# Two-layer graph network: the second layer in steps of eight rows, pairs of rows mixed at once, one-hots per row, four slots for gathered features

## The chip, the cores and the metric

One core of one Trainium2 chip. The metric is the device time of one execution in microseconds, the median of the runs shown. The engines are PE (TensorE, matmuls), DVE (VectorE), ACT (ScalarE), POOL (GpSimd, which here issues the indirect gathers) and SP (SyncE, which issues plain DMAs).

## What is computed

There are 8192 nodes with 128 features and 262144 edges, sorted by target node `dst` (the targets are denser at low numbers). The first layer sums weighted neighbour features, multiplies by W and normalizes. The second one, the subject here, forms for each edge a tensor product of the source node's features with nine edge attributes, sums the products by target node, adds the node's features and normalizes:

```python
edge_index = jnp.stack([src, dst])
x = _layernorm(x + _L0_gnn_ref(x, src, dst, edge_weight, L0_gnn_W), axis=-1)
x = _layernorm(x + _L1_gnn_ref(x, edge_index, edge_attr_9, w0, w1, w2, w3, w4), axis=-1)

# in _L1_gnn_ref: for each of five paths (i1, i2, io)
seg = jnp.einsum('uvw,ijk,eui,evj->ewk', weights[k], _W3J[k], x1s, x2s) * _NORM[k]
out = out.at[:, e:f].add(seg.reshape(E, mo * (2 * lo + 1)))
# then
out = jax.ops.segment_sum(summand, j, num_segments=x.shape[0])
return out / float(np.sqrt(NUM_NEIGHBORS))
```

The product is linear in the features and in each of the nine attributes, so the kernel first sums feature times attribute per target node and attribute, and then multiplies each of the nine sums by a 128x128 matrix (`g.mix[:, m, :]`), which holds the weights and the coupling coefficients.

## The kernel before

The edges are cut into 128 rows of 16 tiles of 128 edges. Function `layer1` runs an outer loop over passes (one pass with these inputs) and in it over the rows. For each row:

- POOL issues 16 indirect DMAs (L1558), one for each tile: 128 feature rows of 512 bytes each land in `feat[z]`, z being one of two row slots. It waits for the ids, which ACT copies to integers for each half row (L1599), and, through `half_summed`, for PE to have read the same half of the row before last.
- SP loads the row's attributes (`attr_in`, L1521), and PE turns them in nine narrow transposes into PSUM (`attr_t`, L1639).
- DVE makes, for each half row of 8 tiles, a one-hot of the target within a window of 16 nodes (`hot`, L1758) and its product with the attributes (`attr_hot`, L1763).
- PE takes the tiles in quads of four. For each quad it zeroes a PSUM bank by a matmul with a zero operand (L1666), and then accumulates one matmul for each tile, features against one-hot times attributes (`quad`, L1673), at a column offset that is read from a table. The last one of a half increments `half_summed`.
- DVE adds the quads of each half to the row's sums in SBUF (`group[z]`, L1784), ACT clears the group for the row after next (L1596).
- PE mixes the nine sums of a row (`mixed`, 9 matmuls of 192 columns, L1688), and DVE adds the result at the row's place to `g.acc` (L1790). This is done in `add_row` while the next row runs.

An f32 matmul leaves two records in the trace, a transpose one. Rows 0 to 111 are in loops of two rows (`Fori(0, EARLY // 2)`); rows 112 to 127 are unrolled, and in 112 to 126 a batch of 512 finished nodes is done beside the edges: four transposes into `y` (L1682) between PE's two halves, which wait for the last row's `add_row`; then DVE's `measure` (L1798 to L1813) and ACT's normalization and store (L1577 to L1584). The last batch follows the last row. Each engine runs its own program in order; the order of the work is that of the code, and semaphores tie the engines together.

Of the kernel before, what the change touches and what calls it, by code (L numbers as in the profile page):

```python
# [89 lines left out]
ROW_SLOTS = 2  # L90
# [36 lines left out]
def constants(n_nodes):  # L127
# [29 lines left out]
    c[:, C_BEGUN] = np.where(done >= 0, BATCH * P * np.minimum(done + 1, n_batches - 1), 0)  # L157
# [18 lines left out]
def gnn_kernel(nc, x, src, dst, attr, weight, w_lin, w_tp, consts, out, tables, x1):  # L176
# [10 lines left out]
    with ExitStack() as ctx:  # L187
# [6 lines left out]
        g.src_col = sb("src_col", [P, g.TN + ROW_SLOTS * ROW_TILES], F32)  # L194
# [41 lines left out]
def setup(nc, g, src, dst, weight, w_lin, w_tp, consts):  # L236

    RN, TN = g.RN, g.TN
    with ExitStack() as ctx:
# [75 lines left out]
        def _(dve):  # L315
# [76 lines left out]
            nc.vector.tensor_copy(g.src_col[:, TN:TN + ROW_SLOTS * ROW_TILES], g.src_col[:, 0:ROW_SLOTS * ROW_TILES])  # L392
# [1024 lines left out]
def layer1(nc, g, x1, attr, out):  # L1417

    RN, TN = g.RN, g.TN
    H, Q, R = HALF_TILES, QUAD_TILES, ROW_TILES  # L1420
    with ExitStack() as ctx:
# [6 lines left out]
        zero_bf = sb("zero_bf", [P, NA * QUAD_WIN], BF16)  # L1428
        off_f = sb("off_f", [P, TN], F32)
        tile_offs = sb("tile_offs", [P, TN // Q, Q - 1], I32)  # L1430
        row_offs = sb("row_offs", [P, RN + 1, Q], I32)
# [6 lines left out]
        quad = ctx.enter_context(nc.psum_tensor("quad", [P, Q, 512], F32))  # L1438
# [11 lines left out]
        EARLY = RN - g.NB  # L1450

        zero_made = sem("zero_made")
# [3 lines left out]
        feat_in = [[sem(f"feat_in{z}_{q}") for q in range(R // Q)] for z in range(ROW_SLOTS)]  # L1456
        attr_here = [sem(f"attr_here{z}") for z in range(2)]
        first_turned = sem("first_turned")
        half_summed = sem("half_summed")
        hot_step = sem("hot_step")  # L1460
        hot_made = sem("hot_made")
        quad_added = sem("quad_added")
        group_zero = sem("group_zero")
        acc_added = sem("acc_added")
# [36 lines left out]
        SUMMED = 2 * RN + 1  # L1501

        def pass_begun(w):

            return w * SUMMED + 2 * ROW_SLOTS

        def all_mixed(w):

            return pass_begun(w) + SUMMED

        def summed(w, r, h):

            return w * SUMMED + r * 2 + (h + 1 + 2 * ROW_SLOTS)

        @block.sync
        def _(sp):
            attr_rows = attr.rearrange("(r t e) m -> r t (e m)", t=R, e=P)

            def load_attr(row, z):

                sp.dma_start(attr_in[z][:], attr_rows[bass.ds(row, 1)].squeeze(0)).then_inc(attr_here[z], 16)  # L1521

            load_attr(0, 0)
            sp.wait_ge(first_turned, 1)
# [7 lines left out]
            with passes(sp) as w:  # L1532
                with sp.Fori(0, EARLY // 2) as i:
                    for z in range(2):
                        sp.wait_ge(half_summed, summed(w, i * 2, z * 2 - 4))
                        load_attr(i * 2 + (z + 1), 1 - z)
                load_x(w, 0)
                for r in range(EARLY, RN):
                    sp.wait_ge(half_summed, summed(w, r - 2, 0))
                    load_attr((r + 1) % RN, (r + 1) % 2)  # L1540
# [3 lines left out]
            for z in range(2):  # L1544
                sp.wait_ge(attr_here[z], n_loads * (8 * RN) + 16 * (1 - z))
# [3 lines left out]
        def _(pool):  # L1549
            with passes(pool) as w:  # L1550
                with pool.Fori(0, RN // ROW_SLOTS) as i:
                    for z in range(ROW_SLOTS):
                        for h in range(2):
                            pool.wait_ge(ids_made, w * (RN * 2) + i * (2 * ROW_SLOTS) + (z * 2 + h + 1))
                            pool.wait_ge(half_summed, summed(w, i * ROW_SLOTS, (z - ROW_SLOTS) * 2 + h))
                            pool.sem_inc(g.turn, 1)
                            for t in range(h * H, h * H + H):
                                pool.indirect_dma_start(  # L1558
                                    feat[z][:, t, :], None, x1,
                                    bass.IndirectOffsetOnAxis(ap=ids[z][h][:, t % H:t % H + 1], axis=0),  # L1560
                                ).then_inc(feat_in[z][t // Q], 16)
                for z in range(ROW_SLOTS):
                    for q in range(R // Q):
                        pool.wait_ge(feat_in[z][q], 16 * Q * (RN // ROW_SLOTS))
                pool.wait_ge(half_summed, all_mixed(w))
                pool.sem_inc(g.turn, 1)
                pool.inc_swdge_sem(sum(feat_in, []), [16 * Q * (RN // ROW_SLOTS)] * (ROW_SLOTS * R // Q), mode="sub")
                pool.sem_inc(landings_cleared, 1)
# [3 lines left out]
        def _(act):  # L1572
            def normalize(w, e):
# [15 lines left out]
            for z in range(ROW_SLOTS):  # L1589
                for h in range(2):  # L1590
                    cols = z * R + h * H
                    nc.scalar.copy(ids[z][h][:], g.src_col[:, cols:cols + H]).then_inc(ids_made, 1)
            with passes(act) as w:
                def clear_and_copy(r, z, e=None):
                    act.wait_ge(half_summed, summed(w, r, -2))
                    nc.scalar.memzero(group[z][:]).then_inc(group_zero, 1)  # L1596
                    for h in range(2):
                        act.wait_ge(half_summed, summed(w, r, h))
                        nc.scalar.copy(ids[z][h][:], g.src_col[:, bass.ds(r * R + (ROW_SLOTS * R + h * H), H)]  # L1599
                                       ).then_inc(ids_made, 1)  # L1600
                        if h == 0 and e is not None:
                            normalize(w, e)

                with act.Fori(0, EARLY // 2) as i:
                    for z in range(2):
                        clear_and_copy(i * 2 + z, z)
                for r in range(EARLY, RN):
                    clear_and_copy(r, r % 2, batch_of(r))
# [17 lines left out]
        def _(pe):  # L1626
            pe.sem_inc(half_summed, 2 * ROW_SLOTS)
            pe.sem_inc(landings_cleared, 1)
            pe.sem_inc(quad_added, R // Q)
            pe.sem_inc(acc_added, 2)  # L1630

            def turn_attr(v, v_half, z):

                pe.wait_ge(attr_here[z], v_half * 16 + 16)
                pe.wait_ge(hot_made, v * 2 + 1)
                pe.sem_inc(g.turn, 1)
                edges = attr_in[z][:].rearrange("t (e m) -> t e m", m=NA)
                for m in range(NA):
                    last = nc.tensor.transpose(attr_t[:, z, m * R:(m + 1) * R], edges[:, :, m],  # L1639
                                               g.cst[0:R, C_IDENT:C_IDENT + R])  # L1640
                return last
# [254 lines left out]
```

## Time and profile before

| | us |
|---|---|
| median of 3 runs | 4115.09 (4114.18 to 4115.81) |
| the profiled execution, its span | 5011.3 |
| PE busy | 3029.2 (60%) |
| POOL busy | 2759.7 (55%) |
| DVE busy | 2089.5 (42%) |
| ACT busy | 1176.6 (23%) |

The profiled execution's own time is its span; no other time of it is given, and it is longer than the timed runs. Up to about 500 us the kernel sorts and prepares, then runs the first layer until 1802, a normalization until 1860, and the second layer from there. Busy shares are averages over these stages.

### The profile page before, as it was taken

To read this page: it belongs to the slowest core of one execution; us is meant where nothing else is said; L and a number is where in the kernel's file an instruction comes from. 1 tells how busy PE (TensorE), PEld (TensorE's weight loads), DVE (VectorE), ACT (ScalarE), POOL (GpSimd) and SP (SyncE) were. 2 spreads that over 40 slices of the span, in tenths; PEclk is the share of its full clock that TensorE was granted. 3 is DMA by queue.
4 is the path that set the end of the run, shared out by engine and by line. 5 is a ranking of instruction groups with operands and counts; after the bars stand their busy time and mean duration, and the time that the engine had idled before them with its cause. 6 is when DMAs were issued, how large, how long until landed. Compare 5 with 4: busy or idle time off the path is not lost.

```text
span 5011.3 us, 63448 instructions
## 1 busy us (share of the span) xinstructions
PE 3029.2 (60%) x18004; PEld 2599.8 (52%) x18006; DVE 2089.5 (42%) x4613; ACT 1176.6 (23%) x2104; POOL 2759.7 (55%) x2887
## 2 busy tenths in 40 slices
PE   2100788888888864555555555555556555555666
PEld 1000778788887863444444444444445444444555
DVE  8999565565565661222222222222222222222333
ACT  5443444444444440000000000000000000000111
POOL 4000555555555536666666666666666666666664
PEclk6555899999999976777777777777777777777666
DMA  1001222222222231111111111111111111111221
GB/s 49 5 11 41 75 71 75 71 71 76 72 71 71 71 96 47 46 47 46 46 46 46 46 47 46 46 46 46 46 47 47 46 47 45 46 46 55 66 66 46
DMA packets 117978, 267.07 MB, mean 53 GB/s; under 512 B 52225, under 2 KB 52369, under 8 KB 116769
## 3 DMA queue, kind: packets, MB, share of 16 engines
q0 software_dynamic: 92080, 191.02, 13.1%
q1 hardware_dynamic: 21234, 66.99, 3.9%
q10 hardware_dynamic: 4608, 8.39, 0.4%
q8 instruction: 25, 0.41, 0.0%
q14 instruction: 31, 0.25, 0.0%
HBM read 251.19 MB, written 8.72 MB: 52 GB/s over the span
## 4 chain that ended last, share of the span: by engine, by line
another core or an unknown queue 34%; PE 11%; issue 10%; DVE 6%; DVEq 2%; ACT 0%; ACTq 0%
PE quad L1673 5%; PE mixed L1688 4%; DVE group L1784 3%; DVE hot L1758 1%; PE quad L1666 1%; PE attr_t L1639 1%; DVE acc L1790 1%; DVEq L1769 1%; DVE attr_hot L1763 0%; DVEq L1784 0%; DVEq L1758 0%; DVEq L1777 0%; DVEq L1780 0%; DVEq L1761 0%
## 5 line engine op out<-in xcount | busy, mean ns | idle before, releaser
L1558 POOL DMA_INDIRECT feat<-x,ids x2048 | 1940.6, 948 | 1181.8 <-issue 615.8
L1784 DVE TENSOR_TENSOR group<-group,quad 128x504 f32 (+1 forms) x512 | 347.3, 678 | 2301.9 <-remote 2167.5
L1134 POOL DMA_INDIRECT l_feat<-in_x,id_of x768 | 737.4, 960 | 916.5 <-ACT w_of L827 368.7
L1673 PE MATMUL quad<-attr_hot,feat 128*128 128x144 f32 x4096 | 842.8, 338 | 547.7 <-issue 544.3
L1673 PEld LDWEIGHTS quad<-attr_hot,feat 128*128 128x128 f32 x4096 | 661.0, 219 | 737.5 <-issue 736.4
L1688 PE MATMUL mixed<-group,mix 128*128 128x192 f32 x2304 | 691.1, 486 | 577.9 <-DVE group L1784 577.9
L1688 PEld LDWEIGHTS mixed<-group,mix 128*128 128x128 f32 x2304 | 650.5, 305 | 622.7 <-issue 556.8
L1599 ACT CAST ids<-src_col 128x8 int32 (+1 forms) x256 | 50.3, 197 | 2746.0 <-remote 2525.4
L1208 PE MATMUL got<-x_near,far_w 128*128 128x128 bf16 x4224 | 341.0, 220 | 160.3 <-issue 148.6
L1208 PEld LDWEIGHTS got<-x_near,far_w 128*128 128x128 bf16 x4224 | 278.7, 98 | 206.4 <-issue 192.1
L1036 DVE TENSOR_SCALAR keys<-swap,src_of,w_of 128x184 f32<-128x184 f32 x1024 | 308.2, 373 | 127.9 <-PE l_pre L1227 122.0
L1036 DVE TENSOR_SCALAR w_row<-swap,src_of,w_of 128x184 f32<-128x184 f32 x1024 | 311.8, 376 | 112.7 <-PE l_pre L1227 108.4
L1763 DVE TENSOR_TENSOR attr_hot<-hot,attr_t 128x1152 f32<-128x1152 f32 x256 | 346.5, 1354 | 9.0
L853 ACT COPY pad<-got 128x640 f32<-128x640 f32 x256 | 176.0, 688 | 595.3 <-remote 450.1
L1227 PE MATMUL l_pre<-w_row,pad 128*128 128x184 f32 x1280 | 297.4, 352 | 0.0
L1227 PE MATMUL l_pre<-keys,pad 128*128 128x184 f32 x1280 | 284.4, 339 | 4.2 <-issue 4.2
L1666 PE MATMUL quad<-zero_bf 1*128 1x504 bf16 x512 | 204.5, 399 | 109.2 <-issue 109.1
L1227 PEld LDWEIGHTS l_pre<-w_row,pad 128*128 128x128 f32 x1280 | 247.0, 216 | 0.0
L1227 PEld LDWEIGHTS l_pre<-keys,pad 128*128 128x128 f32 x1280 | 233.0, 206 | 6.0 <-issue 5.6
L839 ACT ACTIVATE far_keys<-place,turn_f 128x384 bf16<-128x384 bf16 (+2 forms) x384 | 229.1, 630 | 6.5 <-DMA place<-table 6.4
L1227 PE MATMUL l_pre<-w_row,l_feat 128*128 128x184 f32 x768 | 212.6, 362 | 12.6 <-ACT pad L853 7.8
L1227 PE MATMUL l_pre<-keys,l_feat 128*128 128x184 f32 x768 | 203.7, 348 | 20.4 <-ACT pad L853 16.8
(249 smaller groups left out, 2929.8 us busy)
## 6 DMA issues: line engine op xcount, KB each, us to landing
place<-table SPq DMA_DIRECT2D x64, 640.0 KB
feat<-x,ids POOLq DMA_INDIRECT x2048
l_feat<-in_x,id_of POOLq DMA_INDIRECT x768
attr_in<-in_edge_attr SPq DMA_DIRECT2D x129, 72.0 KB
norm_x<-in_x SPq DMA_DIRECT2D x16, 256.0 KB, 2.7
x<-norm_z ACTq DMA_DIRECT2D x16, 256.0 KB, 2.4
x_t<-x SPq DMA_DIRECT2D x15, 256.0 KB
out<-z_t ACTq DMA_DIRECT2D x15, 256.0 KB
```

The lines of the kernel that those rows point to most:

```text
L839: nc.scalar.activation(rest_far[r][:, cols[r]], placed_at(s, j, cols[r]), ACT.Abs, bias=not_wanted[r]).then_inc(far_made, 2 // len(cols))
L853: nc.scalar.copy(rows, got[j % 2][:, 0:NF[j] * P]).then_inc(msg_made, 1)
L1036: made = nc.vector.tensor_scalar(hot_of[(j % 2) * GROUP + i], iota[KIND[j][i]], src_of[s % 2][:, c:c + 1], w_of[s % 2][:, c:c + 1], ALU.is ...
L1134: pool.indirect_dma_start(feat[:, landing, :], None, x, bass.IndirectOffsetOnAxis(ap=id_of[s % 2][:, c:c + 1], axis=0)).then_inc(feat_in[l ...
L1208: last = nc.tensor.matmul(got[z][:, cols], hot, rows, start=(n_done == 0), stop=(n_done == len(products) - 1))
L1227: made = nc.tensor.matmul(pre[:, s % 2, bass.ds(places[i], WIN0)], rows, hot_of[(j % 2) * GROUP + i], start=False, stop=(j == GROUPS - 1 a ...
L1558: pool.indirect_dma_start(feat[z][:, t, :], None, x1, bass.IndirectOffsetOnAxis(ap=ids[z][h][:, t % H:t % H + 1], axis=0),).then_inc(feat_ ...
L1666: nc.tensor.matmul(quad[:, q, 0:NA * QUAD_WIN], zero_bf[0:1, 0:P], zero_bf[0:1, :], start=True, stop=False, skip_group_check=True)
L1673: last = nc.tensor.matmul(bank[:, :, bass.ds(places[t % H], WIN)], feat[z][:, t, :], attr_hot[h][:, t % H, :, :], start=False, stop=(t % Q ...
L1688: last = nc.tensor.matmul(mixed[:, 0:GROUP_WIN], g.mix[:, m, :], group[z][:, m, :], start=(m == 0), stop=(m == NA - 1))
L1763: nc.vector.tensor_tensor(attr_hot[h][:], hot[:].unsqueeze(2).to_broadcast(s4), by_tile[:, h * H:h * H + H, :].unsqueeze(3).to_broadcast(s ...
L1784: nc.vector.tensor_tensor(to, to, quad[:, q, 0:NA * QUAD_WIN].rearrange("p (m n) -> p m n", m=NA), ALU.add).then_inc(quad_added, 1)
```

## The change

Only the second layer changes.

- **Slots and ids.** `feat` has four row slots for two, and one semaphore for each half row (it had one for each quad). The ids are copied for four rows at once. POOL's loop has eight rows.
- **Attributes.** They are loaded for eight rows in one DMA (128 partitions), turned by nine transposes of 128 columns in eight rows (attribute 8 first, in the step of row 2, the other eight in that of row 4), and copied by ACT from PSUM to SBUF (`attr_e`, `attr_next`).
- **One-hots.** One pair of DVE instructions for each row, with all 16 tiles, made two rows ahead into one of two buffers.
- **Zeroing.** ACT clears the two PSUM banks of a half (`clear_half`) as soon as DVE has added them; PE's matmuls with the zero operand are gone, and PE waits for `quad_zero`, once in a half.
- **Mixing.** A group holds two rows; nine matmuls of 384 columns mix both, in the loop after the next row's two halves, in the unrolled rows right after an odd row. DVE adds them with two adds (`add_pair`).
- **Unrolled rows.** The transposes of an even batch wait for all earlier rows, those of an odd batch for one row less (`turn_nodes`), and the node count in `C_BEGUN` is rounded to pairs.

```diff
-ROW_SLOTS = 2
+ROW_SLOTS = 4
+OCTET = 8
+TURN_ROW = 4
+START_LAG = 3
...
-        ids = [[sb(f"ids{z}_{h}", [P, H], I32) for h in range(2)] for z in range(ROW_SLOTS)]
-        feat = [sb(f"feat{z}", [P, R, D], F32) for z in range(ROW_SLOTS)]
-        attr_in = [sb(f"attr_in{z}", [R, P * NA], F32) for z in range(2)]
-        hot = sb("hot", [P, H, WIN], F32)
-        attr_hot = [sb(f"attr_hot{h}", [P, H, NA, WIN], F32) for h in range(2)]
-        group = [sb(f"group{z}", [P, NA, GROUP_WIN], F32) for z in range(2)]
+        ids = [sb(f"ids{b}", [P, O // 2 * R], I32) for b in range(2)]
+        feat = [sb(f"feat{z}", [P, R, D], F32) for z in range(S)]
+        attr_in = sb("attr_in", [O * R, P * NA], F32)
+        attr_e = sb("attr_e", [P, NA, O * R], F32)
+        attr_next = sb("attr_next", [P, O * R], F32)
+        hot = sb("hot", [P, R, WIN], F32)
+        attr_hot = [sb(f"attr_hot{z}", [P, R, NA, WIN], F32) for z in range(2)]
+        group = [sb(f"group{z}", [P, NA, 2, GROUP_WIN], F32) for z in range(2)]
...
+            def clear_half(h):
+
+                nc.scalar.memzero(quad[:, 2 * h:2 * h + 2, 0:NA * QUAD_WIN]).then_inc(quad_zero, 1)
...
+            def half_row(w, r, h, z, n_fill):
+
+                u = w * RN + r
+                places = tile_places(r, h)
+                pe.wait_ge(quad_zero, u * 2 + (h + 1))
+                if h == 0:
+                    pe.wait_ge(hot_made, u + 2)
+                pe.wait_ge(feat_in[z % S][h], n_fill * (16 * H) + 16 * H)
+                pe.sem_inc(g.turn, 1)
+                for t in range(h * H, h * H + H):
+                    bank = quad[:, t // Q, 0:NA * QUAD_WIN].rearrange("p (m n) -> p m n", m=NA)
+                    last = nc.tensor.matmul(bank[:, :, bass.ds(places[t % H], WIN)], feat[z % S][:, t, :],
+                                            attr_hot[z % 2][:, t, :, :], start=False, stop=(t % Q == Q - 1),
+                                            skip_group_check=True)
+                last.then_inc(half_summed, 1)
...
+            def mix(n, side):
+
+                pe.wait_ge(quad_added, n * 8 + 8)
+                pe.wait_ge(acc_added, n * 2 + 2)
+                pe.sem_inc(g.turn, 1)
+                to = mixed[:, 0:2 * GROUP_WIN].rearrange("p (a n) -> p a n", a=2)
+                for m in range(NA):
+                    last = nc.tensor.matmul(to, g.mix[:, m, :], group[side][:, m, :, :], start=(m == 0),
+                                            stop=(m == NA - 1))
+                last.then_inc(pair_mixed, 1)
+
+            def turn_nodes(w, u, e):
+
+                pe.wait_ge(acc_added, u + 2 - e % 2)
...
                 for r in range(EARLY, RN):
...
+                    half_row(w, r, 0, r, r // S)
+                    if batch_of(r) is not None:
+                        turn_nodes(w, w * RN + r, batch_of(r))
+                    half_row(w, r, 1, r, r // S)
+                    if r % 2 == 1:
+                        mix(w * PAIRS + r // 2, r // 2 % 2)
+                    turn_next(w * OCTETS + (r // O + 1), r % O)
...
+            def add_pair(n, starts):
+
+                dve.wait_ge(pair_mixed, n + 1)
+                for half, at in enumerate(starts):
+                    dve.wait_ge(acc_added, n * 2 + (half + 2))
+                    to = g.acc[:, bass.ds(at, GROUP_WIN)]
+                    nc.vector.tensor_tensor(to, to, mixed[:, half * GROUP_WIN:(half + 1) * GROUP_WIN],
+                                            ALU.add).then_inc(acc_added, 1)
```

How the instructions stand, by engine. First PE before, in the unrolled rows, from the last quad of row 113 through its mix and the transposes of the attributes to the transposes of finished nodes in row 114 (`ISA` and `REGISTER_ALU` are register work and waits):

```order
L1666 MATMUL quad<-zero_bf 128x504
L1673 MATMUL quad<-attr_hot,feat 128x9x16
...
L1688 MATMUL mixed<-group,mix 128x192 x9
L1635 ISA
L1639 MATMUL attr_t<-cst,attr_in 128x16 x9
L1650 TENSOR_LOAD tile_offs
L1665 ISA
L1666 MATMUL quad<-zero_bf 128x504
...
L1682 MATMUL y<-cst,acc 128x128 x4
```

The same place of PE after the change, from the transposes of finished nodes in row 115 to the mix of rows 114 and 115 and the start of row 116:

```order
L1749 MATMUL y<-cst,acc 128x128 x4
L1710 TENSOR_LOAD tile_offs
L1720 REGISTER_ALU
L1727 MATMUL quad<-attr_hot,feat 128x9x16
...
L1739 MATMUL mixed<-group,mix 128x384 x9
L1710 TENSOR_LOAD tile_offs
L1720 ISA
L1722 REGISTER_ALU
L1727 MATMUL quad<-attr_hot,feat 128x9x16
```

The zeroing matmuls and the narrow transposes are gone from every row, and a mix of 384 columns stands in every second row where one of 192 stood in each. In DVE's program, two rows of the loop after the change (an even row's one-hots, then the odd row):

```order
L1843 TENSOR_TENSOR hot<-cst,dst_col 128x256
L1847 TENSOR_TENSOR attr_hot<-hot,attr_e 128x2304
...
L1871 TENSOR_TENSOR group<-group,quad 128x9x56
L1878 ISA
L1880 ISA
L1880 TENSOR_TENSOR acc<-acc,mixed 128x192
L1878 REGISTER_ALU
L1880 ISA
L1880 TENSOR_TENSOR acc<-acc,mixed 128x192
```

Both adds into `acc` stand between the two halves of the odd row, and the one-hots are one pair of instructions for each row, where there were two.

## Rows read from the trace of the kernel before

**Rows 1.** The page's head: the span of the profiled execution, one core
```profile
span 5011.3 us, 63448 instructions
```

**Rows 2.** Windows (us, then busy us and instructions by engine, clock, DMA): first layer, second layer's loop
```profile
600.00:1700.00 1100.00, 941.24 (x8170) 886.13 (x8169) 658.23 (x2247) 536.86 (x1101) 630.86 (x658) 0.93 0.22 72
...
1970.00:4628.00 2658.00, 1537.73 (x6879) 1259.54 (x6879) 659.73 (x996) 220.55 (x328) 1658.59 (x1754) 0.71 0.16 47
```

**Rows 3.** Groups in 1970 to 4628: count, busy us, mean ns, idle before and its releasers
```profile
L1558 POOL DMA_INDIRECT feat<-x,ids x1754 | 1659.2, 946 | 999.7 <-issue 515.1 <-ACT ids L1599 303.9 <-PE quad L1673 180.8
...
L1784 DVE TENSOR_TENSOR group<-group,quad 128x504 f32 (+1 forms) x438 | 296.9, 678 | 1998.3 <-remote 1969.2
L1763 DVE TENSOR_TENSOR attr_hot<-hot,attr_t 128x1152 f32<-128x1152 f32 x219 | 296.4, 1354 | 7.6
L1596 ACT ACTIVATE group<-group 128x1728 uint32<-128x1728 uint32 x109 | 179.1, 1643 | 12.2 <-issue 12.2
L1666 PE MATMUL quad<-zero_bf 1*128 1x504 bf16 x437 | 169.3, 387 | 99.2 <-issue 99.1
...
L1758 DVE TENSOR_TENSOR hot<-cst,dst_col 128x128 f32<-128x128 f32 x219 | 62.3, 284 | 0.0
...
L1790 DVE TENSOR_TENSOR acc<-acc,mixed 128x192 f32 x110 | 38.3, 348 | 0.0
```

**Rows 4.** Timeline, POOL, one pause: start us, us, instruction, idle before it
```profile
3217.86 0.95 POOL L1558 DMA_INDIRECT feat<-x,ids  x1 [4.50 <-ACT ids L1599]
...
3219.11 0.95 POOL L1558 DMA_INDIRECT feat<-x,ids  x1 [0.30 <-issue]
```

**Rows 5.** Timeline, PE and DVE, the same row
```profile
3205.00 1.25 PE L1673 MATMUL quad<-attr_hot,feat 128*128 128x144 f32 x8
...
3209.34 0.38 PE L1673 MATMUL quad<-attr_hot,feat 128*128 128x144 f32 x1 [1.13 <-issue]
...
3212.15 0.57 PE L1666 MATMUL quad<-zero_bf 1*128 1x504 bf16 x1 [2.44 <-issue]
...
3216.69 1.49 DVE L1784 TENSOR_TENSOR group<-group,quad 128x504 f32<-128x504 f32 x2 [17.77 <-remote]
```

**Rows 6.** Timeline, POOL's last issue and the last two mixes
```profile
4968.58 0.94 POOL L1558 DMA_INDIRECT feat<-x,ids  x1 [0.30 <-issue]
...
4982.92 4.63 PE L1688 MATMUL mixed<-group,mix 128*128 128x192 f32 x18 [1.77 <-DVE group L1784]
...
4987.48 1.20 PE L1639 MATMUL attr_t<-cst,attr_in 16*128 16x16 f32 x9
...
4990.32 1.25 PE L1673 MATMUL quad<-attr_hot,feat 128*128 128x144 f32 x8
...
4991.70 1.49 DVE L1784 TENSOR_TENSOR group<-group,quad 128x504 f32<-128x504 f32 x2 [7.25 <-PE quad L1673]
...
4991.81 1.25 PE L1673 MATMUL quad<-attr_hot,feat 128*128 128x144 f32 x8
...
4996.75 6.12 PE L1688 MATMUL mixed<-group,mix 128*128 128x192 f32 x18 [2.20 <-DVE group L1784]
```

**Rows 7.** The page's costliest groups: the first layer's gathering matmuls
```profile
L1208 PE MATMUL got<-x_near,far_w 128*128 128x128 bf16 x4224 | 341.0, 220 | 160.3 <-issue 148.6
```

**Rows 8.** The tile feat: POOL's issues, ns min/median/max, first and last start
```profile
L1558 POOL DMA_INDIRECT feat<-x,ids x2048: 942/947/2177, 1859.7 to 4968.6; - x187
```

**Rows 9.** Timeline, PE and DVE in an unrolled row
```profile
4968.79 1.25 PE L1673 MATMUL quad<-attr_hot,feat 128*128 128x144 f32 x8
...
4973.89 1.10 PE L1682 MATMUL y<-cst,acc 128*128 128x128 f32 x4 [3.85 <-DVE acc L1790]
4975.21 0.69 DVE L1798 TENSOR_TENSOR z_t<-x_t,y 128x512 f32<-128x512 f32 x1
...
4976.12 2.29 PE L1673 MATMUL quad<-attr_hot,feat 128*128 128x144 f32 x8
...
4978.03 0.16 DVE L1813 SCALAR_TENSOR_TENSOR shift<-mv,rstd 128x4 f32<-128x4 f32 x1
```

More of the change, by code:

```diff
@@ L1543, in _ @@
             n_loads = sp.value_load(g.n_pass[0:1, 1:2], min_val=1, max_val=g.PASSES1)
-            for z in range(2):
-                sp.wait_ge(attr_here[z], n_loads * (8 * RN) + 16 * (1 - z))
+            sp.wait_ge(attr_here, n_loads * (16 * OCTETS) + 32)
             sp.sem_inc(loads_ended, 1)
@@ L1588, in _ @@
                 act.sem_inc(stored[s], 16)
[L1589 to L1592, printed above, removed]
-            with passes(act) as w:
[L1594 to L1606, printed above, removed]
+            for b in range(2):
+                copy_ids(b, b * (O // 2 * R))
@@ L1692, in _ @@
+                        half_row(w, r, h, j, n_fill)
+                    if j % 2 == 0 and not (first and j == 0):
+                        mix(w * PAIRS + o * (O // 2) + (j - 2) // 2, (j - 2) // 2 % 2)
+                    turn_next(w * OCTETS + o + 1, j)
                 pe.wait_ge(landings_cleared, w + 1)
                 pe.sem_inc(g.turn, 1)
-                with pe.Fori(0, EARLY // 2) as i:
-                    for z in range(2):
-                        row(i * 2 + z, i, z, w * (RN // 2) + i + z)
@@ L1833, in _, with next_hots @@
-                dve.wait_ge(first_turned, 1)
-                hots(w * RN, 0, 0, 0, pass_begun(w))
-                hots(w * RN, 0, 1, 0, pass_begun(w))
-                row(0, 0, first=True)
-                row(0, 1)
-                with dve.Fori(1, EARLY // 2) as i:
-                    row(i, 0)
-                    row(i, 1)
-                for r in range(EARLY, RN):
-                    row(r // 2, r % 2, last=(r == RN - 1))
+                def next_hots(o, j):
+                    if (j + 2) % O == 0:
+                        dve.wait_ge(attr_out, w * (2 * OCTETS) + o * 2 + 4)
+                    r = o * O + (j + 2)
+                    hots(w * RN + r, r, (j + 2) % O, j % 2)
@@ new lines, in row @@
+                def row(o, j, first=False):
+                    r = o * O + j
+                    n = w * PAIRS + o * (O // 2) + j // 2
+                    if j % 2 == 0 or first and j == 1:
+                        starts, offs = [], load_places(r * Q + 1, Q - 1)
+                    else:
+                        begin, *offs, end = load_places(r * Q, Q + 1)
+                        starts = [begin, end]
+                    offs = quad_places(offs)
+                    add_quads(w, r, n, j // 2 % 2, j % 2, 0, offs)
+                    if starts:
+                        add_pair(n - 1, starts)
+                    add_quads(w, r, n, j // 2 % 2, j % 2, 1, offs)
+                    next_hots(o, j)
@@ new lines, in end_pair @@
+                def end_pair(n, r):
+                    begin, *_, end = load_places((r + START_LAG) * Q, Q + 1)
+                    add_pair(n, [begin, end])
+                dve.wait_ge(attr_out, w * (2 * OCTETS) + 2)
+                for r in range(2):
+                    hots(w * RN + r, r, r, r)
+                for j in range(O):
+                    row(0, j, first=True)
+                with dve.Fori(1, LOOPED) as o:
+                    for j in range(O):
+                        row(o, j)
```

295 lines of the change are left out of this document (166 added, 129 removed).

## The prediction, before the change was run

> **What bounds the kernel now.** I began with the busy shares and the stages [rows 1, 2]. The stretch 1970 to 4628 holds 110 rows of the second layer, so a row takes 24.16 us, and the layer is some 3150 us of the 5011.3 us. No engine is full in it: PE 58%, POOL 62%.
>
> Next I read the groups of that stretch and what ended their idle time [rows 3]. POOL's DMA issues take 946 ns each, and 0.30 us lie between two of them [rows 4]. Sixteen issues are so 16 x 1.25 = 20.0 us, of the row's 24.16. The rest is POOL's wait for a free slot: (303.9 + 180.8) / 110 = 4.4 us a row. In the timeline it is the 4.50 us ahead of the issue at 3217.86.
>
> What POOL waits for is PE's first half of the row before last. PE's side is odd [rows 5]. The second quad, the last of that half, starts at 3205.00 and is out by 3206.25. Then PE slows down to a matmul in one to three microseconds (3209.34, 3212.15), and DVE, which waits for the first half alone, is released only at 3216.69, ten microseconds after its last matmul. DVE's 1969.2 us "remote" [rows 3] is this, in every row.
>
> The same row without gathers is the program's last one [rows 6]: POOL's last issue is at 4968.58, the quads follow one another every 1.49 us, DVE starts at 4991.70 as soon as the first half is out, and from mix to mix it is 4996.75 - 4982.92 = 13.8 us. So PE's own chain is 13.8 us, and 24.16 is that plus a stall of some 10 us.
>
> **How the profile stands to the median.** The median is 4115.09, the profiled execution 896 us longer. I use that gap as a measurement. The profiled one can hardly be quicker anywhere, so time has to come out of it. In the first layer PE is busy 941 of 1100 us; its largest idle time there, ahead of the gathers' matmuls and almost all under "issue", is 160 us over the layer [rows 2, 7]. So 736 to 896 us come out of the second layer: 5.75 to 7.0 us a row, and a row in the timed runs is 17.2 to 18.4 us. That is above the 13.8 us chain and below the 20.0 us that POOL's issues take in the profile. Hence I conclude that the ten-microsecond stall is mostly the profile's own, that POOL sets the row in the timed runs, at 1.08 to 1.15 us an issue, and that it does so without waiting for a slot. This is a choice; the rivals drop it.
>
> The Trainium skill (Runtime: NRT & Kernel Launch, The ~15µs preamble/postamble breakdown) gives the profile a kernel-invariant excess of some 6 us over the reported time; by it the stall stands in the timed runs, and the sum would be the profile's, 540 us less. The trace disagrees: the excess is 896 us.
>
> **The change, part by part.**
> *Slots, ids and POOL.* 2048 issues before and after, no other work on POOL; fewer waits (one for ids in four rows, one for a slot in each half). Four slots let POOL run four rows ahead, so its 4.4 us wait goes. In the profiled execution the issues run from 1859.7 to 4968.6 [rows 8]; at 2048 x 1.25 = 2560 us they would end at 4420, and with the 42.7 us behind the last one and 6 us for the end (below) the span is about 4468, 543 less. In the timed runs this wait is not there by the argument above: worth 0 in the 112 looped rows.
>
> *PE.* Out: four zeroing matmuls of 387 ns and nine narrow transposes (1.20 us) a row [rows 3, 6]; in: nine wide transposes in eight rows (four wide ones take 1.10 us [rows 9], so 2.5 us, 0.3 a row), and nine 384-column mixes per pair for eighteen of 192, the same columns. About 2.4 us a row less on PE, and the mix waits every second row only. Hidden behind POOL; worth 2.4 us a row if PE set it.
>
> *DVE.* Four quad adds at 0.68 stay. One-hots: two of 0.284 and two of 1.354 become one of 256 and one of 2304 elements; no row shows these sizes; by elements 3.3 us as before [rows 3], at least 1.6 if the size cost nothing (one of each); I take 3.3. They read an SBUF copy, not PSUM: taken as equal. DVE is busy 6 us in a row; hidden.
>
> *ACT.* New: zeroing 1008 PSUM columns twice a row. The nearest row is 1728 elements in 1.643 us [rows 3], so 0.96 us by elements, 1.64 at most: 1.9 to 3.3 us a row on an engine busy 8%. The group's zeroing doubles in size and halves in number. The copies of the turned attributes are some 1152 columns in eight rows, 0.15 us a row. Behind the zeroing waits the same half of the next row: half-row matmuls 2.3, adds 1.5, zeroing up to 1.6, together 5.4 of a row's 17; hidden.
>
> *The sixteen unrolled rows.* Here is the gain. Before, in rows 112 to 126 the transposes of finished nodes stand between PE's halves and wait for the row's add on DVE, which waits for the first half's adds [rows 9]. With the first half done (4970.0 in that row), the adds take 1.5, the row's add 0.35 [rows 3], the transposes 1.1, and 0.7 lie between them: 3.7 us. PE then runs the second half slowly, 2.29 for 1.25 per quad and 0.6 for 0.38: 2.5 more. The chain is 13.8 + 3.7 + 2.5 = 20.0 us, over POOL's 17.2 to 18.4. Nothing absorbs it with two slots: 15 x (1.6 to 2.8) = 24 to 42 us, less what the last row (13.8 against 17.2 to 18.4) wins back, 3.4 to 4.6: 19 to 39, at 17.8 us 29.
> After, the pair's add is due once in two rows, before the next row's transposes are, and a delay of PE meets slots two rows deeper. The pair's mix has no row: doubled, the mixes of [rows 6] (4.63 and 6.12 us, the clock rising in them) give 9.3 to 12.2; the quads' 1.25 for eight records of 144 columns gives 18/8 x 384/144 x 1.25 = 7.5 at the high level. DVE's chain of a pair is 2 x (3.0 adds + 3.0 measure + 3.3 one-hots) + 0.7 = 19.3, plus a wait of 4.2 to 8.9 for the mix (behind 3.3 of one-hots) and 2.5 to 4.6 for the next half row: 26 to 33 us for two rows, under POOL's 34 to 37. The measure is 4975.21 to 4978.19 [rows 9]. So POOL sets these rows too.
>
> *The start.* ACT clears (two groups 3.3 each, two halves 1 each) ahead of the attributes; first matmuls up to 5 us later, which the four slots hide.
>
> *The end.* After the last landing PE has a whole half instead of a quad (+1.2), the last mix is 7.5 to 12.2 for 6.12 [rows 6] (+1.4 to 6.1; I take 4, since it starts after a pause), and there is a second add of 0.35: +6 in all.
>
> **Sum.** 4115.1 - 29 + 6 = 4092. Its own range, with both ends of each term: 4079 to 4104.
>
> **Rivals.**
> *No change, 0.16.* POOL's issue costs nearly the profile's 1.25 in the timed runs as well. At 20.0 us a row the tail's chain is just hidden, the 29 us are not there, and 4107 to 4123 results. For it: the issue rows are very even. Against: rows of 17.2 to 18.4 from the gap of 896; it needs 345 us out of the part before the second layer.
> *PE sets the row in the timed runs, 0.20.* Some of the stall is real contention with the gathers (the last row, free of it, has no gathers, [rows 6]) and an issue costs only its 0.95 busy us: 15.2 a row. Then rows fall from 17.8 to between 15.2 and 17: 100 to 330 us less, 3785 to 4015, say 3900. Against: PE's unstalled chain of 13.8 is far from 17.2.
> *The stall is wholly real, 0.07.* 543 us less: 3572; scaled by 4115/5011, 3669. Against it is the whole of the gap.
> *Slower, 0.13.* One mechanism: PE has less to do per row, is granted its low level at the end, and there the last chain has the mix at 12.2 for 6.12, two quads at 2.29 for 1.25 (+2) and the wait for the whole half (+1.2): +10 us with the add. It decides when a row costs POOL 20 us or more, so that the tail gives nothing: 4125. The granted clock of 0.71 already in these rows speaks for it [rows 2].
> My case has the remaining 0.44.
>
> **How the numbers follow.** A measurement here can tell about 0.2%, 8 us. Faster: 0.44 + 0.20 + 0.07 = 0.71, less 0.02 for my case's upper edge: 0.69. Same: 0.16 and that 0.02, less 0.01 above: 0.17. Slower: 0.14. The range leaves out the wholly real stall and the lower half of the PE rival, and reaches up over the slow one: 3870 to 4130.
>
> **What would show it.** In the changed kernel's profile: POOL's issues every 1.25 us with waits "<-ACT ids" and "<-PE quad" under 30 us in all, against 485; span near 4470; the unrolled rows at POOL's pace. If PE still stalls with POOL always issuing, four slots only move the wait and the span stays above 4700, which says nothing of the timed runs. If the timed gain is over 100 us, my reading of the gap of 896 us is wrong, and the stall was real; if it is nothing, an issue costs the same in both.

## The result, and the profile after

The changed kernel takes 4328.25 us (median of 4 runs, 4327.1 to 4328.73) against 4115.45 us before in the same session: a ratio of 1.0516, 95% interval 1.0501 to 1.0531. It is slower by 213 us. The forecast was 4092.

The page of the changed kernel: the span, the busy shares, and from its costliest groups those that answer to [rows 3] and [rows 7]. A group has its count, busy us, mean ns of one, and the idle time ahead of it.

```profile
span 4326.9 us, 55226 instructions
...
PE 2405.3 (56%) x15332; PEld 2127.0 (49%) x15334; DVE 2119.9 (49%) x4356; ACT 1420.3 (33%) x2142; POOL 2958.1 (68%) x2887
...
L1562 POOL DMA_INDIRECT feat<-x,ids x2048 | 2147.3, 1048 | 636.6 <-issue 634.4
...
L1871 DVE TENSOR_TENSOR group<-group,quad 128x504 f32 (+1 forms) x512 | 348.0, 680 | 1912.0 <-PE quad L1727 1874.1
...
L1579 ACT ACTIVATE quad<-quad 128x1008 uint32<-128x1008 uint32 x258 | 256.6, 995 | 2031.2 <-DVE group L1871 2031.2
...
L1847 DVE TENSOR_TENSOR attr_hot<-hot,attr_e 128x2304 f32<-128x2304 f32 x128 | 327.5, 2558 | 4.4
...
L1211 PE MATMUL got<-x_near,far_w 128*128 128x128 bf16 x4224 | 301.0, 220 | 10.4 <-ACT far_w L847 10.4
...
L1583 ACT ACTIVATE group<-group 128x3456 uint32<-128x3456 uint32 x66 | 203.3, 3082 | 185.4 <-PE mixed L1739 185.4
```

POOL no longer waits for ids or slots: of its 636.6 us of idle time 12.6 lie ahead of the first issue, and the rest are the 0.30 us between two issues. PE and DVE wait for POOL's data. But one issue takes 1048 ns on average, where it took 946 [rows 3]. POOL is never stopped, and still late: 2048 x 0.1 us is the loss. The tile's rows say that most issues are as before and some are very long (minimum, median, maximum in ns, first and last start):

```profile
L1562 POOL DMA_INDIRECT feat<-x,ids x2048: 940/947/3306, 1529.8 to 4300.1; - x187
```

The timeline shows where a long one stands, POOL and DVE in one row of edges:

```profile
2514.67 1.49 DVE L1871 TENSOR_TENSOR group<-group,quad 128x504 f32 x2 [8.62 <-PE quad L1727]
2515.13 0.95 POOL L1562 DMA_INDIRECT feat<-x,ids  x1 [0.30 <-issue]
...
2516.08 0.42 DVE L1843 TENSOR_TENSOR hot<-cst,dst_col 128x256 f32<-128x256 f32 x1
...
2516.38 0.95 POOL L1562 DMA_INDIRECT feat<-x,ids  x1 [0.30 <-issue]
2516.53 2.56 DVE L1847 TENSOR_TENSOR attr_hot<-hot,attr_e 128x2304 f32<-128x2304 f32 x1
2517.64 2.27 POOL L1562 DMA_INDIRECT feat<-x,ids  x1 [0.30 <-issue]
...
2520.21 0.95 POOL L1562 DMA_INDIRECT feat<-x,ids  x1 [0.30 <-issue]
```

The product `attr_hot` runs from 2516.53 to 2519.09. The gather that POOL was issuing as it started (2516.38) is not touched. The next one, started at 2517.64 while the product runs, ends at 2519.91, 0.82 us after the product. This is so once in every row: 130 of the 2048 issues take over 2 us, of which two stand at the start of the layer, beside DVE's tables, and the other 128, one a row, end 0.81 to 0.83 us behind the end of a product. The product has both inputs in SBUF (`hot`, `attr_e`); before, its second input was the turned attributes in PSUM.

The Trainium skill (SBUF — State Buffer, SBUF: two separate sides) has a rule for this: VectorE and GpSimd share one pair of SBUF ports as an exclusive lock held for a whole instruction, and a VectorE operation with two SBUF inputs takes it only against GpSimd work that reads SBUF. The gather is such work, as it reads its ids from SBUF, and its row agrees; the experiments below test it. One half of the rule doesn't show here. By it whichever of the two starts first blocks the other, but the product at 2516.53 starts inside the issue of 2516.38 to 2517.33 and takes its usual 2.56 us.

The first layer is another surprise. The second layer's first gather starts at 1529.8, not at 1859.7 [rows 8], and the first layer's gathering matmuls wait 10.4 us, not 160.3 [rows 7], though the change doesn't touch that layer.

### The profile page after: what moved, and what is told of

It is laid out like the page before. It is cut to its first block, busy times and chain, and to the rows that moved or that the text cites. A ratio compares the mean times of both kernels' runs of the same rounds, so it can differ in the third digit from the quotient of the medians.

```text
span 4326.9 us, 55226 instructions
## 1 busy us (share of the span) xinstructions
PE 2405.3 (56%) x15332; PEld 2127.0 (49%) x15334; DVE 2119.9 (49%) x4356; ACT 1420.3 (33%) x2142; POOL 2958.1 (68%) x2887
## 4 chain that ended last, share of the span: by engine, by line
POOL 47%; issue 15%; PE 1%; POOLq 0%; DMA 0%; DVE 0%; ACT 0%; DVEq 0%
POOL feat L1562 47%; PE quad L1727 1%; DMA feat<-x,ids 0%; POOLq L1558 0%; PE mixed L1739 0%; POOLq L1559 0%; ACT z_last L1666 0%; POOLq L1552 0%; DVE group L1871 0%; DVE dst_col L1956 0%; DVE z_last L1967 0%; DVE stats L1970 0%; POOLq L1556 0%; POOLq L1510 0%; DVE mv L1973 0%
## 5 line engine op out<-in xcount | busy, mean ns | idle before, releaser
L1562 POOL DMA_INDIRECT feat<-x,ids x2048 | 2147.3, 1048 | 636.6 <-issue 634.4
L1727 PE MATMUL quad<-attr_hot,feat 128*128 128x144 f32 x4096 | 924.9, 409 | 1413.3 <-issue 739.3
L1727 PEld LDWEIGHTS quad<-attr_hot,feat 128*128 128x128 f32 x4096 | 861.8, 295 | 1485.1 <-issue 1482.7
L1579 ACT ACTIVATE quad<-quad 128x1008 uint32<-128x1008 uint32 x258 | 256.6, 995 | 2031.2 <-DVE group L1871 2031.2
L1739 PE MATMUL mixed<-group,mix 128*128 128x384 f32 x1152 | 408.8, 512 | 17.9 <-DVE group L1871 17.9
L1847 DVE TENSOR_TENSOR attr_hot<-hot,attr_e 128x2304 f32<-128x2304 f32 x128 | 327.5, 2558 | 4.4
L1739 PEld LDWEIGHTS mixed<-group,mix 128*128 128x128 f32 x1152 | 232.9, 207 | 167.9 <-issue 43.0
L1211 PE MATMUL got<-x_near,far_w 128*128 128x128 bf16 x4224 | 301.0, 220 | 10.4 <-ACT far_w L847 10.4
L1583 ACT ACTIVATE group<-group 128x3456 uint32<-128x3456 uint32 x66 | 203.3, 3082 | 185.4 <-PE mixed L1739 185.4
L1230 PE MATMUL l_pre<-w_row,pad 128*128 128x184 f32 x1280 | 262.1, 319 | 0.0
```

The source lines that it names most:

```text
L1211: last = nc.tensor.matmul(got[z][:, cols], hot, rows, start=(n_done == 0), stop=(n_done == len(products) - 1))
L1230: made = nc.tensor.matmul(pre[:, s % 2, bass.ds(places[i], WIN0)], rows, hot_of[(j % 2) * GROUP + i], start=False, stop=(j == GROUPS - 1 a ...
L1562: pool.indirect_dma_start(feat[z][:, t, :], None, x1, bass.IndirectOffsetOnAxis(ap=ids[j // (O // 2)][:, c:c + 1], axis=0),).then_inc(feat ...
L1579: nc.scalar.memzero(quad[:, 2 * h:2 * h + 2, 0:NA * QUAD_WIN]).then_inc(quad_zero, 1)
L1583: nc.scalar.memzero(group[n % 2][:]).then_inc(group_zero, 1)
L1727: last = nc.tensor.matmul(bank[:, :, bass.ds(places[t % H], WIN)], feat[z % S][:, t, :], attr_hot[z % 2][:, t, :, :], start=False, stop=(t ...
```

## The experiments

All times below are compared with the kernel before on the same chip in the same session: 4111.05 us (the runs up to the product in the kernel before, and the changed kernel with two slots), 4111.11 us (the halves and the first three kernels with 8 gathers) and 4111.29 us (the other two with two slots).

**The kernel before once more.** No edit.

> The kernel before, unchanged, profiled once more. Theory (the profile of 5011 us was stretched by the recording itself: PE's semaphore posts come up to tens of microseconds after its last matmul there and 14 ns after in the profile of the changed kernel, and the second layer starts at 1860 us there and at 1530 here): if this execution is recorded without that, its span is near 4115, the first gather of the second layer is near 1530, POOL issues one every 1.25 us, a row takes 20.0 us (2048 x 1.25 = 2560 us in all), and DVE's and POOL's waits for PE are gone. If it is recorded with it, the span is again near 5000 and rows take 24.2 us while the timed execution stays at 4115. Rival (what the prediction assumed: the first layer is nearly as long as profiled and an issue costs 1.08 to 1.15 us outside the profile): an undisturbed profile would show first gather near 1700 and issues every 1.08 to 1.15 us.

Measured: 4111.52 us timed, and a profile without the disturbance. Its page:

```profile
span 4109.7 us, 63449 instructions
...
L1558 POOL DMA_INDIRECT feat<-x,ids x2048 | 1937.5, 946 | 636.4 <-issue 621.1
```

The tile feat (minimum, median, maximum, first and last start):

```profile
L1558 POOL DMA_INDIRECT feat<-x,ids x2048: 940/944/2175, 1528.8 to 4089.1; - x187
```

A window of the first layer, in which PE is busy 800 of 800 us:

```profile
600.00:1400.00 800.00, 800.00 (x7977) 787.59 (x7976) 679.80 (x2196) 534.19 (x1073) 604.92 (x640) 1.00 0.30 96
```

And DVE's adds in one row of edges, in the timeline:

```profile
2505.12 1.49 DVE L1784 TENSOR_TENSOR group<-group,quad 128x504 f32<-128x504 f32 x2 [7.50 <-PE quad L1673]
```

So the execution that the prediction was read from was 902 us longer than this one: 331 before the second layer (1859.7 - 1528.8), 549 between its first and last issue (3108.9 against 2560.3), 22 behind it. Whether its recording stretched it or it really ran that long isn't shown; no timed execution of this kernel was over 4117.23 us. One part of the expectation missed: DVE's waits for PE aren't gone (1689.2 us over the program); they are now put down to PE's quads, not to "remote", as DVE idles until POOL's data have come and been multiplied. And 2560.3 / 2047 = 1.251 us: in the undisturbed kernel before, POOL issues without a pause at the profile's own 1.25 us, 20.0 us a row. There was nothing in the second layer to gain from slots or from PE.

**The product's input.** The changed kernel with the one-hot in PSUM:

```diff
-        hot = sb("hot", [P, R, WIN], F32)
...
         y = ctx.enter_context(nc.psum_tensor("y", [P, BATCH * P], F32))
+        hot = y[:, 0:R * WIN].rearrange("p (t n) -> p t n", t=R)
...
                 pe.wait_ge(x_used, w * NE + e + 2)
+                pe.wait_ge(hot_made, u + 3)
```

> The changed kernel with the one-hot written to the PSUM bank y instead of SBUF, so that the product of 2304 elements reads one input from PSUM and one from SBUF; in the unrolled rows the transposes of finished nodes wait for the one-hots made before them. Same sizes, same loops, same slots. Theory: the 133 gathers of over 1.1 us, 210 us together, go: 4328 - 210 = 4118, between 4105 and 4135, and every gather takes 0.95 us. Rivals (loop of eight rows, four slots, attribute load, ACT's clears, or the length of the product rather than where it reads): stays at 4328 within 15 us. If only a part of the loss comes from the product, it ends between.

Measured: 4117.18 us (10 runs), ratio 1.0016 (1.0006 to 1.0025). The timeline of POOL and DVE beside a product of the same size and the same length:

```profile
2521.43 0.94 POOL L1562 DMA_INDIRECT feat<-x,ids  x1 [0.30 <-issue]
2521.53 2.56 DVE L1848 TENSOR_TENSOR attr_hot<-y,attr_e 128x2304 f32<-128x2304 f32 x1
2522.68 0.95 POOL L1562 DMA_INDIRECT feat<-x,ids  x1 [0.31 <-issue]
2523.93 0.95 POOL L1562 DMA_INDIRECT feat<-x,ids  x1 [0.30 <-issue]
```

Two gathers start while the product runs, and neither is held. In the whole program 258 do, and none of them takes over 0.96 us. Seven issues are still over 1.0 us: four beside DVE's tables at the start, and three beside the one-hot instruction itself, which still reads two SBUF tiles (at most 1.17 us). These few lines give back 207 of the 213 us. The loop of eight rows, the slots, the large attribute load and ACT's clears are all still there, so none of them is the cause; nor is the product's length.

**The same in the kernel before.** Its product reads a constant tile in SBUF; the true attributes are left out.

```diff
+        attr_s = sb("attr_s", [P, NA * R], F32)
...
+            nc.vector.memset(attr_s[:], 0.5).then_inc(attr_s_made, 1)
...
-                by_tile = attr_t[:, z, 0:NA * R].rearrange("p (m t) -> p t m", m=NA)
+                by_tile = attr_s[:].rearrange("p (m t) -> p t m", m=NA)
```

> The kernel before, with one operand of its two attribute products of each row (1.35 us each) read from a constant tile in SBUF in place of the turned attributes in PSUM; it leaves out the true attributes. Theory (a VectorE product with both inputs in SBUF holds up the gather that POOL is issuing until it ends): a product of 2.56 us costs POOL 1.65 us in the changed kernel, that is all but 0.9 us of it; of two products of 1.35 us some 0.45 us each remain, 0.9 us a row, 128 rows: 4115 + 115 = 4230, at least 4170, at most 4290 if hardly anything of a product passes beside a gather. In its profile one or two gathers a row are over 1.1 us and end 0.8 us after a product. Rivals (the eight-row loop, four slots, the 576 KB attribute load, ACT's clears of PSUM): none of them is in this kernel, so 4115 and gathers of 946 ns throughout.

Measured: 4203.38 us, ratio 1.0229 (1.0212 to 1.0247), 92 us more. One of its holds:

```profile
2511.38 1.36 DVE L1767 TENSOR_TENSOR attr_hot<-hot,attr_s 128x1152 f32<-128x1152 f32 x1
2512.08 1.48 POOL L1560 DMA_INDIRECT feat<-x,ids  x1 [0.30 <-issue]
2513.86 0.95 POOL L1560 DMA_INDIRECT feat<-x,ids  x1 [0.30 <-issue]
```

The gather at 2512.08 ends at 2513.56, 0.82 us after the product's end at 2512.74. So the operand alone brings the loss into the old kernel. It costs less than the 115 us expected, 0.36 us a product. The size of a hold follows from these rows: 0.82 us plus what is left of the product when the gather starts, less the usual 0.95. A gather starts every 1.25 us, so a product of 1.36 us holds one gather for anything from nothing to 1.2 us, by how the two fall together, and one of 2.56 us always holds one for 1.2 to 2.4 us.

**The product in two halves.** The changed kernel, both inputs in SBUF:

```diff
-                s3, s4 = [P, R, WIN], [P, R, NA, WIN]
+                s3, s4 = [P, R, WIN], [P, H, NA, WIN]
...
-                nc.vector.tensor_tensor(attr_hot[z][:], hot[:].unsqueeze(2).to_broadcast(s4),
-                                        by_tile.unsqueeze(3).to_broadcast(s4), ALU.mult).then_inc(hot_made, 1)
+                for h in range(2):
+                    t = slice(h * H, h * H + H)
+                    done = nc.vector.tensor_tensor(attr_hot[z][:, t], hot[:, t].unsqueeze(2).to_broadcast(s4),
+                                                   by_tile[:, t].unsqueeze(3).to_broadcast(s4), ALU.mult)
+                done.then_inc(hot_made, 1)
```

> The changed kernel with the product made in two instructions of 1152 elements, one right after the other, both inputs in SBUF as before. Theory (a gather that begins while a product runs is held until that one instruction ends, and goes on 0.8 us longer, part of it beside the next product): the first product holds one gather for 0.6 us on average, the next gather begins near the end of the second product and is held little; 0.6 to 0.8 us a row, 77 to 100 us: 4190 to 4215, near the kernel before with a constant in SBUF (4203), and about half of the loss gone. Rival (what counts is the total time of two-SBUF-input work beside the gathers, held through both): 4325.

Measured: 4181.05 us, ratio 1.0170 (1.0153 to 1.0187), 70 us more than before, a little below the range of the theory and 144 from the rival's figure. Two products, shown as one group of 2.62 us, and the gather beside them:

```profile
1621.80 2.62 DVE L1849 TENSOR_TENSOR attr_hot<-hot,attr_e 128x1152 f32<-128x1152 f32 x2
1622.14 1.83 POOL L1562 DMA_INDIRECT feat<-x,ids  x1 [0.30 <-issue]
...
1624.28 0.96 POOL L1562 DMA_INDIRECT feat<-x,ids  x1 [0.30 <-issue]
```

The gather ends at 1623.97, before the second product does (1624.42): it is held by the first alone. What holds the gather is let go between two instructions that follow one another at once.

**Two slots.** The changed kernel with `ROW_SLOTS = 2`, and then the same with the one-hot in PSUM.

> The changed kernel with two row slots for gathered features instead of four; nothing else differs. Theory: slots have no part in the loss. POOL sets the row at 21.6 us in the looped rows and PE's work of a row pair is below that, so 4328 within 10 us; up to 4360 if the unrolled rows now wait for slots. Rival (POOL running four rows ahead is what slows it, through more transfers in flight or landings beside PE's reads): below 4250.

> The changed kernel with the one-hot in PSUM and two row slots instead of four. Theory (POOL never waits for a slot in an undisturbed execution, with two slots or with four): 4117, within 6 us, and waits of POOL for PE under 30 us in all. Rival (the four slots give something that the 4.4 us a row of the first profile promised): 4130 or more.

Measured: 4321.33 us (ratio 1.0510, 1.0492 to 1.0527), and 4117.39 us (1.0015, 1.0006 to 1.0024), which is the time with four slots. Four slots neither cost nor give anything here.

**The account.** The pages' sums of POOL's issues, against the 1937.5 us of the kernel before, beside the measured times:

| kernel | issues, busy us | more than before | time, more than before |
|---|---|---|---|
| changed | 2147.3 | 209.8 | 212.8 |
| changed, two slots | 2140.7 | 203.2 | 210.3 |
| before, constant in SBUF | 2030.5 | 93.0 | 92.3 |
| changed, halves | 2001.2 | 63.7 | 69.9 |
| changed, one-hot in PSUM | 1940.8 | 3.3 | 6.1 |
| the same, two slots | 1937.0 | -0.5 | 6.1 |

The time follows the issues in each, and the changed versions have 3 to 7 us on top, which the version of the kernel before hasn't. (The first row is from the session of the result, the others from the sessions named above.)

**What hides behind POOL.** Three kernels with 8 gathers in a row instead of 16; the matmul of each odd tile takes the features of the even one, so half of the source rows are left out. The counts that the waits for landings go by are halved to match. The cut below is of the gathers' loop and of the changed kernel's matmul.

```diff
-                            for t in range(h * H, h * H + H):
+                            for t in range(h * H, h * H + H, 2):
...
-                    last = nc.tensor.matmul(bank[:, :, bass.ds(places[t % H], WIN)], feat[z % S][:, t, :],
+                    last = nc.tensor.matmul(bank[:, :, bass.ds(places[t % H], WIN)], feat[z % S][:, t // 2 * 2, :],
```

> The kernel before with 8 gathers in a row for 16: each tile's matmul takes the features that landed for the even tile, so half of the source rows are left out. Theory (2048 issues of 1.25 us set the second layer in the timed runs): with 10.0 us of issues a row the next limit is PE's chain, 13.8 us by the last row of the first profile, up to 15.2: 4111 - 128 x (4.8 to 6.2) = 3320 to 3500, and some 90 more for the transposes in the unrolled rows, 3400 to 3590. Rival (the rows of 20.0 us are PE's own chain): stays above 4050.

> The changed kernel with the one-hot in PSUM (4117) and 8 gathers in a row, the other half of the source rows left out as in the run of the kernel before with 8. Theory (the parts of the change do shorten PE's chain, by the zeroing matmuls, narrow transposes and the wait for the mix, and this is hidden behind the gathers): PE has some 10.3 us of work in a row, so rows of 10.5 to 12.5 us, 4117 - 128 x (7.5 to 9.5) = 2900 to 3160, at least 200 us below the kernel before with 8 gathers. Rival (the change shortens nothing outside POOL): equal to that within 50 us.

> The changed kernel as it is (one-hot in SBUF) with 8 gathers in a row, the other half of the source rows left out. Theory (the product holds a gather, which costs time only where POOL's issues set the row): POOL has 10.0 + 1.65 = 11.65 us a row; where PE's row is 12 us or more, this equals the run with the one-hot in PSUM within 30 us; where PE's row is 10.5, it is up to 150 us above. Rival (the product in SBUF costs PE, DVE or the landing directly, not POOL's issue): 200 us above it, as with 16 gathers.

Measured: 3375.75, 2882.30 and 3096.48 us (ratios 0.8213, 0.7011 and 0.7530, each within 0.0014). The groups of the gathers on the three pages, in this order:

```profile
L1558 POOL DMA_INDIRECT feat<-x,ids x1024 | 970.4, 948 | 845.2 <-ACT ids L1599 553.2
```

```profile
L1562 POOL DMA_INDIRECT feat<-x,ids x1024 | 971.2, 948 | 331.5 <-issue 314.3
```

```profile
L1562 POOL DMA_INDIRECT feat<-x,ids x1024 | 1215.5, 1187 | 324.3 <-issue 317.3
```

With half of the issues the kernel before needs (970.4 + 845.2) / 128 = 14.2 us a row; POOL waits, and PE's chain sets the row, close to the 13.8 of the forecast. The changed kernel without the hold needs 10.2, still POOL's pace. So the change does shorten the chain of PE, DVE and ACT by at least 4 us a row, 493 us over the program, and with 16 gathers all of it lies behind 20.0 us of issues. Both times lie a little below the ranges expected, 3375.75 for 3400 to 3590 and 2882.30 for 2900 to 3160.

With the hold it is 12.0 us a row and 214 us more. Here my expectation missed: it had at most 150 us, for PE's row being 10.5, and in the looped rows PE keeps up with POOL's 10.2. The issues are 244.3 us longer (1215.5 - 971.2), and 214 of them are paid. Most of the rest is at the end, where without the hold PE is further behind POOL: from the last issue to the end of the span it is 62.0 us without the hold and 43.2 with it. The 214 is near the 200 of the rival, by which the product costs PE, DVE or the landing directly. The figure alone doesn't settle it; the issues do: 127 of them end 0.81 to 0.83 us behind the end of a product, and the product itself takes 2559 ns here and 2557 with its one-hot in PSUM.

**The same with two slots.**

> The changed kernel with the one-hot in PSUM, 8 gathers in a row (half of the source rows left out), and two row slots instead of four; with four it was 2882, the kernel before with 8 gathers 3376. Theory (the 494 us between these come from PE's shorter chain: zeroing, transposes, mix every second row): most of it stays, 2882 to 3000. Rival (they come from the slots): above 3250.

Measured: 2881.26 us. Not even with half of the issues do four slots give anything; the gain is in PE's chain.

## Why the prediction was wrong, by its own steps

**The step that failed** is the one on DVE: "They read an SBUF copy, not PSUM: taken as equal", and "hidden". For DVE it is equal: 2.56 us for 2 x 1.354 [rows 3], and 0.42 for 2 x 0.284. The cost is on POOL, the engine that I had just found to set the row, and I asked only how long the instruction takes, not what it keeps another engine from. It costs 210 us. Without this loss the forecast would still have been 29 us off: with the one-hot in PSUM the change measures 6 us slower, where I had 23 faster; that is the second step, below. The trace of before had the mechanism in it. [Rows 8] give a maximum of 2177 ns beside a median of 947, and I didn't ask which issues these were. They are the first ones, beside DVE's table instructions (POOL and DVE of the kernel before, the profile of 5011.3 us):

```profile
1859.34 1.75 DVE L1736 TENSOR_TENSOR off_f<-tile_start 128x1536 f32<-128x1536 f32 x1
1859.74 2.18 POOL L1558 DMA_INDIRECT feat<-x,ids  x1 [12.62 <-issue]
...
1861.67 1.03 DVE L1739 TENSOR_SCALAR tile_offs<-off_f,keep 128x1536 int32<-128x1536 f32 x1
1862.22 1.29 POOL L1558 DMA_INDIRECT feat<-x,ids  x1 [0.30 <-issue]
...
1864.30 1.52 DVE L1743 TENSOR_SCALAR off_f<-tile_start,keep 128x2048 f32<-128x2048 f32 x1
1865.08 1.55 POOL L1558 DMA_INDIRECT feat<-x,ids  x1 [0.31 <-issue]
1865.85 2.29 DVE L1744 TENSOR_TENSOR dst_col<-dst_col,off_f 128x2048 f32<-128x2048 f32 x1
...
1866.93 2.03 POOL L1558 DMA_INDIRECT feat<-x,ids  x1 [0.30 <-issue]
```

The gathers end at 1861.92, 1863.51, 1866.63 and 1868.96, each 0.81 to 0.83 us after the DVE instruction that was running as it started (1861.09, 1862.70, 1865.82, 1868.14). With this rule on the product of 2.56 us, and 1.2 to 2.4 us of hold a row, the forecast would have been 150 to 310 us more.

**The gap of 896 us** was the second wrong step. That the stall is not in the timed runs was right. Placing the gap was wrong: I bounded what comes out of the first layer by one group's idle time of 160 us [rows 7], and it was 331: the last gathering matmul of that layer ends at 1796.8 in the first profile and at 1465.9 in the second. Idle time couldn't bound it, since busy time was stretched too. The window of 600 to 1400 in the first profile, to be set beside the 7977 PE instructions in 800 us above:

```profile
600.00:1400.00 800.00, 683.89 (x5938) 644.41 (x5937) 479.66 (x1636) 390.98 (x801) 459.22 (x479) 0.93 0.22 72
```

PE is busy for 85% of the window but gets through 74% of the instructions. With 331 us out of the part before the second layer, the row of the timed runs is 20.0 us and not 17.2 to 18.4, and an issue costs 1.25 in both. The rival "no change" had this right, and named the 345 us that it needs.

**The sixteen unrolled rows** hence had no 29 us to give. In the second profile of before they run at POOL's pace: the 255 steps between the last 256 issues take 318.6 us, 1.25 each.

**PE, slots, ACT.** The slots worth nothing: right, shown with 16 and with 8 gathers. PE's part hidden: right, and larger than the 2.4 us a row that I had worked out, at least 4. ACT's clears of 1008 columns: 995 ns, in the range of 960 to 1640 and near the choice by elements, and hidden.

**The end, +6 us:** right in size, and in part by luck. From the last issue to the end of the span the changed kernel has 4326.9 - 4300.1 = 26.8 us for 4109.7 - 4089.1 = 20.6, so 6.2 more; with the one-hot in PSUM it has 4119.2 - 4093.9 = 25.3. The last mix before (second profile), and with the one-hot in PSUM:

```profile
4096.10 5.25 PE L1688 MATMUL mixed<-group,mix 128*128 128x192 f32 x18 [2.20 <-DVE group L1784]
```

```profile
4102.66 6.04 PE L1739 MATMUL mixed<-group,mix 128*128 128x384 f32 x18 [1.99 <-DVE group L1872]
```

In the changed kernel the last mix, at 4308.72, takes 7.74 us. So the mix gave 0.8 to 2.5 us where I took 4. The 6.04 us were at a mean granted clock of 1.00, under my 7.5 for the high level, so scaling the quads' time by columns gave too much. Behind the mix 10.5 us follow for 8.4, 2.1 more where I had only the 0.35 of a second add. The two errors nearly cancel.

**The rivals.** The slower one was right in sign alone: the last quads do run at a granted clock of 0.50, but in the kernel before too (second profile), and the mix of 12.2 us didn't come. Its 10 us are not the 213. The true mechanism was not on the list. Of my signs, POOL's waits for ids and slots under 30 us came true; "issues every 1.25 us" failed in the trace once a row; and the span is 4326.9, not near 4470, since this profile has no stretch in the first layer.

**A version that beats both** isn't among these. The changed kernel with the one-hot in PSUM is the best of its kind and equals the kernel before within 0.2%; both stand at 2048 issues of 1.25 us. It is the one to keep if issues get fewer: with 8 a row it is 15% faster than the kernel before.

## What to carry to other kernels

Find the engine that sets the pace, and then ask of each moved operand on every other engine what it keeps that engine from, not only how long it takes: where POOL issues DMAs without a pause, a long DVE instruction should have one input in PSUM (cutting it in two took two thirds of the loss away). Look at the maximum of the pacing instruction beside its median, and find what ran beside the long ones. When the profiled execution is far longer than the timed ones, don't share out the gap: a second profile of the unchanged kernel settles it.

## What the runs showed of the hardware that was not expected

- A gather's issue that starts while a DVE instruction with both inputs in SBUF runs is held until 0.81 to 0.83 us after that instruction's end; one in progress when the instruction starts isn't lengthened (2516.38, 0.95 us, above). An undisturbed issue is 0.95 us, so by difference some 0.13 us of it would be done ahead of the wait; no row shows that directly. The Trainium skill (SBUF — State Buffer, SBUF: two separate sides) has the lock for the instruction's length, and the halves show it released between two instructions.
- One streamed input in SBUF was enough in two cases, TENSOR_SCALARs over 1536 and 2048 f32 elements (L1739, 1.03 us, and L1743, 1.52 us, above), whose other operand is one column (`keep`). It isn't always: in the first layer of the second profile of before, gathers that start with 0.34 us of a TENSOR_SCALAR of 184 elements left (L1036) take 0.94 to 0.95 us. The same page names, beside two SBUF inputs, VectorE's perf modes that use both ports; no run here shows which mode these instructions were in.
- Short instructions hold little: the one-hots of the kernel before (0.28 us, two SBUF inputs) make 22 of its 2048 issues longer than 1.0 us, none longer than 1.06.
- The product with its one-hot in PSUM takes 2557 ns, in SBUF 2558: the place of this input doesn't show on DVE at all.
- Two profiles of one program were 5011.3 and 4109.7 us long, with medians of timed executions of 4111 to 4115. The stretched one shows itself by idle time "<-remote" on DVE (1969.2 us [rows 3]) and by pauses of PE under "issue" between matmuls [rows 5]. Why the first was so long stays open.
